# Soft mixture of experts behind attention: one order for all slot steps, spare products at step 2, four buffers among the experts, combine's first weights in halves

## The reference, cut to what matters

```python
h = patches @ tok_W.T + tok_b; h = concat([h, txt])            # 32 x 113 tokens of 256 values
h = h + attention(layernorm(h))                                  # 16 heads, rope
x = layernorm(h)
logits = (x @ phi_w.T + phi_b).reshape(tokens, 64 experts, 32 slots)
D = softmax(logits over slots); Cw = softmax(logits over experts)
X_tilde = einsum('tnp,td->npd', D, x)                            # sums over all 3616 tokens
X_tilde = tanh(layernorm(clip(X_tilde)))
Y_tilde = einsum('npd,ndH->npH', X_tilde, expert_w) + expert_b
out = h + einsum('tnp,npH->tH', Cw, Y_tilde)
```

## Time and profile before

| | us |
|---|---|
| median of 3 runs | 931.06 (931.0 to 931.23) |
| the profiled execution | 939.2 |
| its span, first to last instruction | 937.5 |
| mean granted TensorE clock | 0.98 of full speed |

### The profile page before, as it was taken

How to read it: one execution, slowest core, us unless ns; L and a number is a source line. 1 busy time by engine, 2 the same in 40 slices (tenths; PEclk the granted TensorE clock), 3 DMA queues, 4 the chain that set the end, 5 groups by cost and what they waited for, 6 DMA issues and landing times.

```text
span 937.5 us, 21735 instructions
## 1 busy us (share of the span) xinstructions
PE 909.0 (97%) x7668; PEld 748.2 (80%) x7668; DVE 720.4 (77%) x1083; ACT 493.0 (53%) x793; POOL 529.2 (56%) x512
## 2 busy tenths in 40 slices
PE   8989999999999899999999999999999989999997
PEld 7777887888886567888888888888888648888885
DVE  3577777777874888999999999999998745555552
ACT  1255555554554356676676666766765453333331
POOL 1275333223231377999999999999998551001000
PEclk9999999999997979999999999999999989999999
DMA  7601111111111254423223233232256975776750
GB/s 247 211 27 45 44 42 41 42 40 44 44 47 36 60 104 157 134 64 102 75 78 101 60 91 86 65 101 77 76 149 250 378 265 201 244 241 224 236 185 18
DMA packets 99925, 110.98 MB, mean 118 GB/s; under 512 B 12216, under 2 KB 91156, under 8 KB 93860
## 3 DMA queue, kind: packets, MB, share of 16 engines
q1 hardware_dynamic: 97760, 106.23, 36.9%
q0 software_dynamic: 1376, 3.70, 1.1%
q10 hardware_dynamic: 740, 0.41, 0.1%
HBM read 72.06 MB, written 38.21 MB: 118 GB/s over the span
## 4 chain that ended last, share of the span: by engine, by line
PE 90%; POOL 4%; DVE 3%; issue 2%; ACT 1%; DVEq 0%; ACTq 0%; POOLq 0%
PE slots_p_sum L1430 22%; PE slots_logits L1461 16%; PE slots_p_turn L1571 11%; PE slots_p_turn L1579 6%; PE attend_p_qk L568 5%; PE slots_p_turn L1415 5%; PE attend_p_row L568 4%; PE attend_p_score L549 3%; PE attend_p_score L540 3%; PE attend_p_k L560 3%; PE embed_acc L148 3%; PE attend_p_qk L577 2%; PE attend_p_k L555 1%; PE attend_p_q L555 1%; PE slots_logits L1540 1%
## 5 line engine op out<-in xcount | busy, mean ns | idle before, releaser
L1430 PE MATMUL slots_p_sum<-slots_x,slots_disp 128*128 128x256 f32 (+1 forms) x928 | 214.5, 387 | 0.1
L1430 PEld LDWEIGHTS slots_p_sum<-slots_x,slots_disp 128*128 128x128 f32 (+1 forms) x928 | 173.6, 192 | 31.7 <-issue 9.6
L1167 POOL TENSOR_TENSOR slots_comb<-slots_comb,slots_cmax 128x1024 f32<-128x1024 f32 x56 | 108.0, 1948 | 14.0 <-DVE slots_cmax L963 12.4
L1571 PE MATMUL slots_p_turn<-slots_y_parts,slots_hi 128*128 128x512 f32 (+1 forms) x464 | 111.0, 391 | 0.3 <-DVE slots_lo L1100 0.3
L446 POOL TENSOR_TENSOR attend_stack<-attend_rope_a,attend_rope_b 113x128 f32<-113x128 f32 x128 | 54.4, 456 | 87.0 <-DVE attend_rope_b L396 87.0
L1179 POOL TENSOR_TENSOR slots_comb<-slots_comb,slots_csum 128x2048 f32<-128x2048 f32 x27 | 97.8, 3620 | 5.7 <-DVE slots_csum L940 5.7
L1571 PEld LDWEIGHTS slots_p_turn<-slots_y_parts,slots_hi 128*128 128x128 f32 (+1 forms) x464 | 84.0, 186 | 18.5 <-DVE slots_lo L1100 0.8
L1172 POOL TENSOR_TENSOR slots_disp<-slots_disp,slots_dsum 128x2048 f32<-128x2048 f32 x27 | 98.5, 3648 | 0.0
L1218 POOL DMA_DIRECT2D out<-slots_o x29 | 15.9, 547 | 142.4 <-DVE slots_o L1095 142.4
L950 DVE TENSOR_TENSOR slots_disp<-slots_logits,slots_dmax 128x512 f32<-128x512 f32 x112 | 77.5, 692 | 4.6
L1461 PE MATMUL slots_logits<-phi_hi,slots_xt_hi 128*128 128x512 f32 x224 | 77.1, 425 | 1.1 <-ACT slots_comb L1282 1.1
(11 more groups left out here) (164 smaller groups left out, 1854.9 us busy)
## 6 DMA issues: line engine op xcount, KB each, us to landing
combine_t<-slots_ct SPq DMA_DIRECT2D x224, 128.0 KB, 2.4
slots_comb<-combine_t SPq DMA_DIRECT2D x14, 1024.0 KB, 5.3
slots_ct<-combine_t SPq DMA_DIRECT2D x14, 1024.0 KB, 5.6
slots_spare_w<-wexp SPq DMA_DIRECT2D x6, 1024.0 KB, 6.3
slots_disp<-wexp SPq DMA_DIRECT2D x6, 1024.0 KB, 6.6
expert_w<-wexp SPq DMA_DIRECT2D x4, 1024.0 KB, 10.6
h<-attend_h_out SPq DMA_DIRECT2D x32, 113.0 KB
slots_h_t<-h SPq DMA_DIRECT2D x28, 128.0 KB, 2.3
```

The source lines that it names most:

```text
L1167: nc.gpsimd.tensor_tensor(m, m, cmax[0:rows, shalf(i)].unsqueeze(2).broadcast_to([rows, SLOTS // 2, EXPERTS]), ALU.subtract).then_inc(csub ...
L1430: last = nc.tensor.matmul(p_sum[u % 2][:, i, :], disp[d][part].rearrange("p n s -> p (n s)")[:, 128 * block:128 * block + 128], x[d][part] ...
L1571: return nc.tensor.matmul(p_o[c % 2][0:rows], hi[c % 2][:, e, 0:rows], y_parts[:, e].rearrange("p i c -> p (i c)"), start=e == 0, stop=e = ...
```

## The change

It makes three edits.

- **Opening.** Step 1 gets the order that the later steps have. PE turns tile 2 inside `rest`, before attention's last projection, so step 1 starts with its group, then the short tile's turn, and the logits woven. ACT's copy of the turned tile moves behind the second bank's copy, with a wait for tile 1's logits; `keep_sum` of unit 0 follows it, ahead of banks 2 and 3; the short tile's quarter and the other `keep_sum` follow the dispatch exponentials, and the combine exponentials come last. DVE takes bank 2 before `low_turned`. At step 2 PE does eight spare products of `ident` with itself, whose result nothing reads, before the group.
- **Experts.** Four `y` buffers (the two of before and combine's two output tiles `o`), so `add_bias(i)` waits for `low_part(i-4)`; POOL's `low_part(2u-8)` and `(2u-7)` stand behind `deviation(u)` from u = 4.
- **Combine's first weights.** The first two tiles' splits are done in halves, spread over the last blocks; the second tile's weights go to another buffer (`ct[1]`) and are loaded ahead of expert weights 14 and 15, behind a wait for tile 27's stores (`ct_st[1]`).

```diff
-    y = [t[:] for t in h_t]
+    y = [t[:] for t in h_t + o]
+    YRING = len(y)
-    raw = ([... comb[i] ... for i in (1, 0)] + [ct[i][:] for i in (1, 0)])
+    raw = [of for i in (1, 0) for of in (as_weights(comb[i]...), ct[i][:])]
 SP:
         for i in range(WRING, EB):
             load_expert(i)
+            if i == EB - 3:
+                sp.wait_ge(ct_st[1], CT_STORES * 16 * (TILES // 2))
+                load_weights(1, 1, 128)
         store(LAST, LAST % 2)
-        load_weights(1, 1, 128)
-        sp.wait_ge(ct_st[1], CT_STORES * 16 * (TILES // 2))
 DVE, step:
+            opening = static(t) and t == 1
+            if opening:
                 short_sum()
+                dispatch_in(t, c, rows, 2)
...
-            wait_for(dve, y_lo_ok, i - 1)
+            wait_for(dve, y_lo_ok, i - YRING + 1)
...
+        def first_low_weights(n, i):
+            dve.wait_ge(first_hi_ok, 2 * n + i + 1)
+            ...
+            last = nc.vector.tensor_tensor(lo[n][:, part], raw[n][:, part], hi[n][:, part].bitcast(F32), ALU.subtract)
...
-            if i >= EB - 4 and i % 2:
-                low_weights((i - EB + 3) // 2, (i - EB + 3) // 2, 128)
+            if i >= EB - 6 and i % 2:
+                first_low_weights((i - EB + 5) // 4, (i - EB + 5) // 2 % 2)
+        first_low_weights(1, 1)
 POOL:
-            if u >= 5:
-                low_part(2 * u - 10)
-                low_part(2 * u - 9)
+            if u >= 4:
+                low_part(2 * u - 8)
+                low_part(2 * u - 7)
 ACT, step:
+            def high_turned():
+                act.wait_ge(xt_ps_ok, val(t + 2))
+                if opening:
+                    act.wait_ge(logit_ok, 2 * NB)
+                nc.scalar.activation(xt_hi ...)
+            if nxt and not opening:
+                high_turned()
...
+                    if opening and b == 1:
+                        high_turned()
-                    if units and not filling and b == 1:
+                    if units and b == 1:
                         keep_sum(*units[0])
...
+            if m >= UNITS - 3:
+                first_high_weights((m + 3 - UNITS) // 2, (m + 3 - UNITS) % 2)
 PE:
+            if nxt and not (static(t) and t == 1):
+                turn_x(t, c, nrows)
+            if static(t) and t == 2:
+                keep_clock()
+            multiply_group(t, c)
...
+        def keep_clock():
+            for i in range(8):
+                nc.tensor.matmul(p_turn[1][:, i % 4, :], ident[:], ident[:], start=True, stop=True)
...
             multiply_logits(0, 128, [1])
+            turn_x(1, 1, 128)
             project_out(BATCH - 1)
```

More of the change, by code:

```diff
@@ L725, in slots @@
     as_weights = lambda t: t.rearrange("p (b c) -> p b c", c=128)
-    raw = ([as_weights(comb[i][:].rearrange("p s n -> p (s n)")) for i in (1, 0)] + [ct[i][:] for i in (1, 0)])
+    raw = [of for i in (1, 0) for of in (as_weights(comb[i][:].rearrange("p s n -> p (s n)")), ct[i][:])]
     h_res = [x[i] for i in (5, 6, 7, 0)]
     o = [sb(f"o{i}", [128, C]) for i in range(2)]
+    y = [t[:] for t in h_t + o]
+    YRING = len(y)
     p_o = [p_turn[i][:].rearrange("p b c -> p (b c)") for i in range(2)]
@@ L990, in step @@
                 low_turned(t + 1)
-            dispatch_in(t, c, rows, 2)
+            if not opening:
+                dispatch_in(t, c, rows, 2)
             dispatch_in(t, c, rows, 3)
@@ L1101, in low_weights @@
                                     ALU.subtract).then_inc(lo_ok, 1)
+        def first_low_weights(n, i):
+            dve.wait_ge(first_hi_ok, 2 * n + i + 1)
+            if n == 0 and i == 0:
+                dve.wait_ge(sum_ok, FINAL + UNITS)
+            part = slice(EB // 2 * i, EB // 2 * (i + 1))
+            last = nc.vector.tensor_tensor(lo[n][:, part], raw[n][:, part], hi[n][:, part].bitcast(F32), ALU.subtract)
+            if i == 1:
+                last.then_inc(lo_ok, 1)
         for i in range(2 * UNITS - 8, EB):
             add_bias(i)
-            if i >= EB - 4 and i % 2:
-                low_weights((i - EB + 3) // 2, (i - EB + 3) // 2, 128)
+            if i >= EB - 6 and i % 2:
+                first_low_weights((i - EB + 5) // 4, (i - EB + 5) // 2 % 2)
+        first_low_weights(1, 1)
         def low_part(n, turn, c, rows):
@@ L1204, in low_part @@
             pool.wait_ge(y_hi_ok, i + 1)
-            nc.gpsimd.tensor_tensor(y_lo[:, i], y[i % 2], y_hi[:, i].bitcast(F32), ALU.subtract).then_inc(y_lo_ok, 1)
+            nc.gpsimd.tensor_tensor(y_lo[:, i], y[i % YRING], y_hi[:, i].bitcast(F32), ALU.subtract).then_inc(y_lo_ok, 1)
         for u in range(UNITS):
             deviation(u)
-            if u >= 5:
-                low_part(2 * u - 10)
-                low_part(2 * u - 9)
-        for i in range(2 * UNITS - 10, EB):
+            if u >= 4:
+                low_part(2 * u - 8)
+                low_part(2 * u - 7)
+        for i in range(2 * UNITS - 8, EB):
             low_part(i)
@@ L1261, in step @@
             units = [] if own_sums(t) else sums(t, c)
-            filling = static(t) and t <= 1
+            opening = static(t) and t == 1
             def exp_half(buf, cut, before, per, done, i):
@@ L1291, in step @@
                     exp_half(disp[c % RING], nhalf, dsub_ok, 2, dexp_ok, 1)
-            if live and filling:
-                for i in range(2):
-                    exp_half(comb[c % 2], shalf, csub_ok, 1, cexp_ok, i)
             if weights:
@@ L1297, in step @@
                 keep_quarter(t - 1, (c + 1) % 2, half(-1), 1)
-                if units and not filling:
+                if units:
                     keep_sum(*units[1])
             for i in range(2):
-                if live and not filling:
+                if live:
                     exp_half(comb[c % 2], shalf, csub_ok, 1, cexp_ok, i)
@@ L1304, in step @@
                     keep_quarter(t - 1, (c + 1) % 2, half(-1), 2 + i)
-            if units and filling:
-                for s, u in units:
-                    keep_sum(s, u)
         def rest(keep_values, high):
@@ L1342, in high_part, with first_high_weights @@
             act.wait_ge(y_ok, i + 1)
-            nc.scalar.activation(y_hi[:, i], y[i % 2], ACT.Copy).then_inc(y_hi_ok, 1)
+            nc.scalar.activation(y_hi[:, i], y[i % YRING], ACT.Copy).then_inc(y_hi_ok, 1)
         def high_weights(n, turn, c, rows):
             act.wait_ge(w_ld[c], val(16 * (turn + 1)))
-            if static(n) and n < 2:
-                act.wait_ge(sum_ok, FINAL + UNITS)
             wait_for(act, mm_ok, n - 1)
             nc.scalar.activation(hi[c % 2][:, :, 0:rows], raw[c][:, :, 0:rows], ACT.Copy).then_inc(hi_ok, 1)
+        def first_high_weights(n, i):
+            act.wait_ge(w_ld[n], 16)
+            act.wait_ge(sum_ok, FINAL + UNITS)
+            part = slice(EB // 2 * i, EB // 2 * (i + 1))
+            nc.scalar.activation(hi[n][:, part], raw[n][:, part], ACT.Copy).then_inc(first_hi_ok, 1)
         tanh(0)
@@ L1467, in step @@
             nrows = rows_of(t + 1)
-            if nxt:
[L1469 to L1482, removed]
+            if nxt and not (static(t) and t == 1):
[3 more added lines that the diff above has]
+            multiply_group(t, c)
+            turn_weights(t - 1, c + 1, 0)
+            turn_weights(t - 1, c + 1, 1)
+            for q in (2, 3):
+                if nxt:
+                    multiply_logits(t, nrows, [q - 2])
+                turn_weights(t - 1, c + 1, q)
+            if nxt:
                 multiply_logits(t, nrows, [2, 3])
+        def keep_clock():
+            for i in range(8):
+                nc.tensor.matmul(p_turn[1][:, i % 4, :], ident[:], ident[:], start=True, stop=True)
         def short_logits(b, columns):
```

11 lines of the change are left out of this document (4 added, 7 removed).

## The result

Over 20 runs each the changed kernel has a median of 930.43 us (927.87 to 934.31) and the kernel before 936.24 (931.0 to 939.24). The ratio is 0.9944, 95% interval 0.9928 to 0.9961, so some 5.2 us less (3.7 to 6.7). The forecast was 5.45 us less.

The account below looks back on a forecast made before the run. PE, busy 97% of the span, was taken as the bound, losing time only in waits or at low clock. Opening +2.85 and experts -8.3 gave -5.45 us, so median 931.06 becomes 925.6, range 920.8 to 929.8.

Parts of the forecast that it names:

- the last of the sum: Whole kernel: the 5.45 us difference, taken off the median 931.06 as the same in a faster run, gives 925.6.
- ACT's wait for attention's last store: Opening, step 1: ACT's first keep_sum stands from 317.9 to 322.6, so DVE's maxima start 2.85 us later.
- the gate: Step 2: PE's second product of the group, waiting for tile 1's dispatch weights; forecast at 334.05 instead of 331.2.
- The clock behind the gate: Step 2: after PE idles about 4.6 us the clock falls again, staying low 13.65 us as before.
- The spare products: Step 2: eight float32 products, 16 instructions, take 1.8 us ahead of the gate and cost nothing.
- Experts: products(6) to combine: waits 5.7, first combine 0.3, low clock 2.8, less 0.5, so 8.3 us won.
- ACT's longer list: Experts: with a half split, ACT needs 3.3 us per two blocks against PE's 2.74; 0.5 us lost.
- The queue of SP: Experts: new wait stands behind stores already landed at 740.2; moved 1 MB load costs nothing, cover 3 us.
- Rival 1: Opening: ACT stands but the clock holds; tile 2's chain sets gate 3; total -9.0, 922.1 us; chance 0.18.
- gate 3: Step 3: PE's next such wait, for tile 2's dispatch weights; about 348.6 if the clock holds, against 349.4 before.
- Rival 3: Opening: store lands before ACT asks, the gate at 329.8, clock holds; total -13.6, 917.5 us; chance 0.10.
- Rivals 2, 4 and 5: Opening's low spell doubles, 932.5, chance 0.05; SP's wait held, 933.9, 0.06; experts' clock falls or ACT gaps, 928.5, 0.11.

Follow-up runs that it names:

- e1: The kernel before, unchanged, run again 12 times: median 937.04 us, ratio 0.998 to before.
- e2: The kernel before with only the edits among the experts and of combine's first weights, opening as before: 926.7 us, ratio 0.9887 to before.
- e8: e4 with SP loading tile 4's rows ahead of the experts' bias and of the wait for attention's last store: 926.2 us, ratio 0.9877 to before.
- e5: The whole change, unchanged, run again: 932.04 us, ratio 0.9952 to before.
- e4: The whole change with unit 0's keep_sum in step 1 moved behind the dispatch exponentials and the short tile's quarter: 926.3 us, ratio 0.9881 to before.
- e6: The whole change without the eight spare products at step 2: 931.6 us, ratio 0.9936 to before.
- e7: The whole change with 24 spare products at step 2 instead of 8: 926.4 us, ratio 0.9902 to before.
- e9: e8 with 16 spare products instead of 8: 924.1 us, ratio 0.9884 to before.
- e12: e2 (old opening, new experts) with 12 spare products at step 2 ahead of turn_x: 927.1 us, ratio 0.9896 to before.
- e10: The kernel before with only the four y buffers and POOL's earlier low_part, one profile: products(6) to first combine 18.13 us, before 26.7.
- e3: The kernel before with only the opening's edits, experts as before: 939.6 us, ratio 1.0019 to before.

## Why the prediction was right or wrong

**The step that failed is the last of the sum:** the difference was taken off 931.06, "for attention, where most of such scatter could lie, is not touched". The profiled execution stood 8.1 us above those three runs; I called it scatter, kept the level of the three, and gave the range nothing for it. e1 shows what it mostly goes with. Before's executions spread over 9 us, for the most part with the time that the clock is low, at 0.40 us a microsecond, and 931 is the lower edge; 47 of the 78 lie above 937. Taken off the median of 20, 936.24, the same difference gives 930.8, against 930.43. A range that knew of the spread would have reached to 935. A sign of it was there: the profile's mean clock of 0.98 is some 37 us at the low level, and an execution 8 us faster could hardly have had as much. Why three executions in a row lay at the edge isn't known, and it may be chance; to take them for the level was the mistake.

The reason given for it was half right. Attention does hold a large part of the scatter: its last store is issued 4.6 us apart between profiles (310.46 in e2, 315.04 in e8), with the same instructions but for the two transposes. And between executions with the same spells in attention the sum comes out: the profile of before has a span of 937.5, that of e5 932.2, forecast 932.0. But taking the difference "to be the same in a run that is 8.1 us faster" fails. The lowest of the changed kernel's 32 executions is 927.87, the lowest of before's 98 is 931.0: 3.1 us at the edge, not 5.45. No execution of the changed kernel reached 925.6. No execution of before near 931 was profiled, so which part of the gain is smaller there stays open; the low spell among the experts, from which 2.8 us of the forecast gain came, is the first suspect.

**ACT's wait for attention's last store: right.** Predicted: ACT stands until 7.8 us after the issue, DVE's maxima 2.85 us later, the gate 19.2 us after the issue instead of 16.4. Measured: 19.6, 3.2 us later. The missing 0.35 lies in ACT's restart, 0.33 us of issue behind the landing. The prediction took the 7.7 us of this store from the trace without asking what made them; the last section shows it. e4 shows the cause by the opposite edit: with the `keep_sum` moved behind the copies the gate is at 14.9.

**The clock behind the gate: right**, 13.65 us again in both profiles of the changed kernel and step 2 ending 3.4 us late (2.85 predicted). e6 and e7 show that the gap brings it down. That the gap is the only cause is not shown: in e9 and e12 it fell with gaps of 0.29 and 0.79 us.

**The spare products: right.** 1.88 us from the first to the next instruction (1.8 predicted), hidden ahead of the gate, and too few: e6.

**Experts: right, a term too small.** Predicted 8.3, measured 8.81 us. The term is ACT's longer list, put at 0.5 us; PE's wait for ACT in the profile after is 0.2. The sum without it was 8.8. The 8.81 is against one profile of before; its stretch wanders by 1.3 us between profiles, so the agreement to a tenth is luck, while the end of the new stretch, 0.5 us earlier than forecast, repeats. e10 shows that the buffers make nearly all of it. The queue of SP did as said: tile 27's stores were long in, and no wait of PE for expert weights appears.

**The rivals.** Rival 1's mechanism shows in e7: with the clock held behind the gate, tile 2's chain gives gate 3 at 33.76 us after the store; the prediction had 348.6 - 314.8 = 33.8. Rival 3's shows in e4 and e8, with the gate at 14.9 to 15.0 (15.0 predicted), but its price was too high: about 11 us less than before instead of 13.6, since the clock didn't hold in most runs. Rivals 2, 4 and 5 did not come: no spell behind the gate was longer than 13.65 us, SP's moved wait cost nothing, and the clock stayed at 1.00 among the new experts.

**What a better version is.** e2, e4, e7, e8, e9 and e12 lie at 0.988 to 0.990 of before, 4 to 7 us ahead of the change, and can't be told from each other. The simplest is e2: leave the opening as it was.

## What to carry to other kernels

Before an instruction with a wait is moved forward in an engine's list, look at when that wait really ends, also where the profile shows none: its old place hid it, and another engine's wait for the same event may show the time. Count the level of a kernel over enough runs to see the spread of its granted clock, and forecast a difference; three runs that agree within 0.3 us can all be at the edge. Spare products ahead of a known gate are no sure gain: 8 in a gap of over 4 us did nothing, 24, which filled it, gave 4 to 5 us back, and filling gaps of 2.1 us (e9) and 2.75 us (e12) gave nothing that could be measured.

## What the runs showed of the hardware that was not expected

- The last store of attention, 113 KB in 113 rows, took 7.7 us from issue to landing, and SP's wait for it was 7.5 us in all twelve profiles with SP's old order, with the DMA engines at a share of 0.07. That share is about one engine of the 16, and the trace's packets agree: from 314.5 to 322.2 us of before they are of 1 KB and start one after another, one every 42 ns with a single pause (24 GB/s). 113 of them take 4.8 us. Counted back from the last packet, at 7.4 us behind the issue, the store's own begin at 2.6; until then the packets are those of transfers issued before it, attention's store of 4.1 us earlier above all. The landing is seen at 7.7. The window over the last store's own packets, before:

```profile
317.40:322.20 4.80, 3.98 (x17) 3.29 (x18) 4.37 (x8) 3.24 (x7) 0.74 (x2) 1.00 0.07 24
```

- Size alone doesn't make this. The combine weights' stores, also issued by SP, are 128 KB and land after 2.4 us in the median; this row of section 6 of the page is the same before and after:

```profile
combine_t<-slots_ct SPq DMA_DIRECT2D x224, 128.0 KB, 2.4
```

  The Trainium skill's page "DMA: Bandwidth & Descriptors", section "Anatomy of one DMA", has a fit, for DMAs that GpSimd issues, by which an estimate is 2.3 us for the 113 KB. The combine stores come near it, attention's last store doesn't. The 113 rows against 128 partitions are the difference that meets the eye; no run here changes them.
- Three runs of one kernel within 0.3 us of each other and 20 with a spread of 8 us are no contradiction: the mean clock of single executions of before lay between 0.978 and 0.988.
- The clock fell in e9 2.65 us behind a gap of only 0.29 us, in a stretch of float32 products of which half have 32 rows, and in e12 1.6 us behind the end of one of 0.79. In e7 it didn't, in the one profile taken. What makes the difference stays open.
- The longer PE had stood ahead of the gate, the longer the clock was low behind it: 13.65 us after gaps of 4.4 to 4.8 us (after, e5, e6) and after 2.75 at `turn_x` (the five profiles with the old opening and no spare products), 10.2 after 3.04 (e3), 6.8 and 10.2 after 2.08 (e4, e8), 6.8 after 0.79 and 0.29, none after no gap (e7). These are single executions; it is an order seen, not a rule tested.
